# Cross attention: scores of two units as two 64-row products side by side, in place of one 128-row product per unit

## The chip, the cores and the metric

The kernel runs on one core of a Trainium2 chip. The metric is the device time of one execution in microseconds (us), as the median of several runs.

Engines: TensorE (PE in the profile, and PEld for its weight loads), VectorE (DVE), ScalarE (ACT), GpSimd (POOL) and SyncE (SP), which issues transfers.

## The reference, cut to what matters

A decoder of two layers on 8 batches of 256 tokens with 256 features. Each layer has a self mixing part (window attention, then a recurrence), a cross attention over 77 context rows, and a feed-forward part (experts, then a binarized one); each part is followed by a residual sum and a layer norm. Only the two cross attentions are changed. Both compute:

```
Q = (x @ Wq + bq)      # 16 heads of 16 features
K = (ctx @ Wk + bk)    # ctx: 77 rows of 256
V = (ctx @ Wv + bv)
scores = einsum('bhqd,bhkd->bhqk', Q, K) / sqrt(16)    # masked
attn = softmax(scores)
x = layernorm(x + (attn @ V) @ Wo + bo)
```

## The kernel before, in words

`cross_attention` is called twice, for layer 0 and layer 1. It loops over the batches 0 to 7. Batch 0 and batch 7 are written out; the six between are three turns of a loop that holds an odd and an even batch. A batch has 8 units (`UNITS`), `c` = 0 to 7. A unit is 128 of the batch's 256 tokens and 4 of the 16 heads (`UH` = 4): units 0 to 3 are the first 128 tokens, 4 to 7 the second.

Queries and keys lie transposed: features on the 128 partitions, in two halves `g` of 8 heads each. A head has 16 features, so the heads of a product for 4 heads need only 64 of the 128 partitions. The keys are kept once per head in `km`, multiplied by 1 on the head's own 16 partitions and by 0 elsewhere (`mask_keys` on GpSimd). A score product takes 128 partitions of `q` as weights and 4 heads x 77 columns of `km` as the moving operand; the other heads' partitions meet zeros. The operands are fp32, and each fp32 product shows in the profile as two records.

The steps of a unit, by engine:

- TensorE `score` (L1200): scores of 4 heads, 128 x 308, into `s_bank[c % 2]`.
- VectorE `mask_scores` (L1076 in layer 0, L1074 in layer 1) from the bank to `z`; `take_maximum` (L1082).
- GpSimd `subtract` (L953).
- ScalarE `power` (L1017): the exponential, to `probs`.
- TensorE `turn_probs` (L1209): four transposes into a `t_bank`.
- ScalarE (L1025) and VectorE `probs_rest` (L1087) read it out as a high and a low f16 part, `pth` and `ptl`.
- TensorE `weigh` (L1223): the product with the values.

The order on each engine is written out by hand, and every engine works its queue in that order. TensorE's order for unit `c` is: `turn_probs(c)`, `score(c + 2)`, the shared step of slot `c`, `weigh(c - 1)`. VectorE's is: mask of `c + 2`, `probs_rest(c)`, maximum of `c + 2`, then other work. ScalarE's is: copy of turned `c`, exponential of `c + 1`, then the shared step. For `c` = 6 and 7 the scores are those of units 0 and 1 of the next batch.

The shared steps go by slot (`CA`): slot 0 the keys of the next batch (L1175), slot 1 its values (L1179), slot 2 the transposed heads (L1184) and slot 3 the output product (L1189) of the previous batch's second 128 tokens, slot 4 the transposed tokens of the next batch (L1163, read out to `xt` by ScalarE L995), slot 5 its query product (L1169, read out to `q` by ScalarE L998), slots 6 and 7 heads and output of the batch's first 128 tokens.

Window attention, earlier in the kernel, is not changed. Its `score` first writes a band mask with 128-row bf16 products (L678) and then adds fp32 products on 32 rows each (L684), in turn on the four groups of 32 rows; its `weigh` (L714) uses 128 rows again.

Of the kernel before, what the change touches and what calls it, by code (L numbers as in the profile page):

```python
# [27 lines left out]
P = 128  # L28
# [134 lines left out]
def first(b):  # L163

    return isinstance(b, int) and b == 0
# [44 lines left out]
def window_attention(nc, x_dram, xt_dram, wqkv_dram, wo_dram, rope_dram, ident, half, X, next_loads):  # L210
# [561 lines left out]
CTX = 77  # L772
CH, CD = 16, 16
UH = 4
UNITS = TPB * CH // UH
MASKED = -4.0e9
OPEN = 1.0e38
# [11 lines left out]
    first=[("key", 0), ("value", 0), ("tokens", 0), ("query", 0)],  # L789
# [25 lines left out]
def cross_attention(nc, weights, ctx_dram, ident, half, X, next_loads=None, table=None):  # L815
    tag, additive = weights.tag, weights.additive
    w, bias, rows, mask = weights.w, weights.bias, weights.rows, weights.mask
    with ExitStack() as ctx:
# [14 lines left out]
        q = [sb(f"q{k}", [P, KT_, SEQ]) for k in range(2)]  # L833
        kb = sb("kb", [P, KT_, CTX])
        km = [sb(f"km{k}", [P, KT_, CH // KT_, CTX]) for k in range(2)]
        v = sb("v", [P, CH, CD])
        vh = [sb(f"vh{k}", [P, CH, CD + 1], F16) for k in range(2)]
        vl = [sb(f"vl{k}", [P, CH, CD + 1], F16) for k in range(2)]
        z = [sb(f"z{k}", [P, UH, CTX]) for k in range(2)]
        top = sb("top", [P, 2, UH])  # L840
        probs = [sb(f"probs{k}", [P, UH, CTX]) for k in range(2)]
        pth = [sb(f"pth{k}", [P, UH * P], F16) for k in range(2)]
        ptl = [sb(f"ptl{k}", [P, UH * P], F16) for k in range(2)]
        inv = sb("inv", [P, TPB, CH])
# [5 lines left out]
        s_bank = [ctx.enter_context(nc.psum_tensor(f"{tag}_scores{k}", [P, 512], F32)) for k in range(2)]  # L850
# [15 lines left out]
        scores = sem("scores")  # L866
        masked = sem("masked")
# [63 lines left out]
        def _(pool):  # L931
# [18 lines left out]
            def subtract(b, c):  # L950
                pool.wait_ge(maxed, b * UNITS + c + 1)
                k = c % 2
# [93 lines left out]
        def _(dve):  # L1046
            for k in range(2):
                dve.memset(vh[k][:, :, CD:CD + 1], SCALE)
                ins = dve.memset(vl[k][:, :, CD:CD + 1], 0.0)
# [15 lines left out]
            def mask_scores(b, c):  # L1065

                k = c % 2
                dve.wait_ge(scores, b * UNITS + c + 1)
                if not (first(b) and c < 2):
                    dve.wait_ge(exped, b * UNITS + c - 1)  # L1070
                s = s_bank[k][:, 0:UH * CTX].rearrange("p (h k) -> p h k", h=UH)
                m = at(mask if additive else limit, b * TPB + c // (UNITS // TPB)).unsqueeze(1).broadcast_to((P, UH, CTX))
                if additive:
                    ins = dve.scalar_tensor_tensor(out=z[k][:], in0=s, scalar=CD ** -0.5, in1=m, op0=ALU.mult, op1=ALU.add)  # L1074
                else:
                    ins = dve.tensor_tensor(z[k][:], s, m, ALU.min)  # L1076
                ins.then_inc(masked, 1)
# [75 lines left out]
        @block.tensor  # L1153
        def _(pe):
            def step(b, par, kind, i, bank, uses):
                dst = shared[bank]
                if not (isinstance(uses, int) and uses == 0):
                    pe.wait_ge(free[bank], uses)
                if kind == "tokens":
                    pe.wait_ge(staged[par], 8 * (b - par) + 16)  # L1160
                    for g in range(KT_):
                        for t in range(TPB):
                            ins = pe.transpose(dst[:, g * SEQ + t * P:g * SEQ + (t + 1) * P],  # L1163
                                               xs[par][:, t, g * P:(g + 1) * P], ident[:])
                elif kind == "query":
                    wait_read(pe, [("tokens", 0)], b)
                    for g in range(KT_):
                        for k in range(KT_):
                            ins = pe.matmul(dst[:, g * SEQ:(g + 1) * SEQ], w[:, 0, k, g * P:(g + 1) * P], xt[par][:, k],  # L1169
                                            start=(k == 0), stop=(k == KT_ - 1))  # L1170
                elif kind == "key":
                    pe.wait_ge(context_loaded[par], 8 * (b - par) + 16)
                    for g in range(KT_):
                        for k in range(KT_):
                            ins = pe.matmul(dst[:, g * CTX:(g + 1) * CTX], w[:, 1, k, g * P:(g + 1) * P],  # L1175
                                            context[par][:, k], start=(k == 0), stop=(k == KT_ - 1))
                elif kind == "value":
                    for k in range(KT_):
                        ins = pe.matmul(dst[0:CTX, 0:DIM], context[par][:, k], w[:, 2, k],  # L1179
                                        start=(k == 0), stop=(k == KT_ - 1))  # L1180
                elif kind == "heads":
                    pe.wait_ge(normed, b * TPB + i + 1)
                    for g in range(KT_):
                        ins = pe.transpose(dst[:, g * P:(g + 1) * P],  # L1184
                                           o[:, i, g * 8:(g + 1) * 8].rearrange("p h d -> p (h d)"), ident[:])
                else:
                    wait_read(pe, [("heads", i)], b)
                    for g in range(KT_):
                        ins = pe.matmul(dst[:, 0:DIM], ot[:, i, g], w[:, 3, g], start=(g == 0), stop=(g == KT_ - 1))  # L1189
                ins.then_inc(full[bank], 1)  # L1190

            def score(b, c, par):
                t, part = divmod(c, UNITS // TPB)
                g, h = part // 2, UH * (part % 2)
                if c == 0:
                    wait_read(pe, [("query", 0)], b)
                    pe.wait_ge(key_masked, (b + 1) * KT_)
                if not (first(b) and c < 2):
                    pe.wait_ge(masked, b * UNITS + c - 1)
                pe.matmul(s_bank[c % 2][:, 0:UH * CTX], q[par][:, g, t * P:(t + 1) * P],  # L1200
                          km[par][:, g, h:h + UH].rearrange("p h k -> p (h k)"), start=True, stop=True).then_inc(scores, 1)

            def turn_probs(b, c):
                k = c % 2
                pe.wait_ge(exped, b * UNITS + c + 1)
                if not (first(b) and c < 2):
                    pe.wait_ge(probs_low, b * UNITS + c - 1)
                for h in range(UH):
                    ins = pe.transpose(t_bank[k][0:CTX, h * P:(h + 1) * P], probs[k][:, h], ident[:])  # L1209
                ins.then_inc(probs_t, 1)  # L1210

            def weigh(b, c, par):
                k, t = c % 2, c // (UNITS // TPB)
                pe.wait_ge(probs_low, b * UNITS + c + 1)
                if c == 0:
                    pe.wait_ge(v_low, b + 1)
                if c % (UNITS // TPB) == 0 and not first(b):
                    pe.wait_ge(normed, b * TPB + t - 1)
                for h in range(UH):
                    head = UH * (c % (UNITS // TPB)) + h  # L1220
                    cols = slice(h * P, (h + 1) * P)
                    for n, (a, x) in enumerate(((pth[k], vh[par]), (pth[k], vl[par]), (ptl[k], vh[par]))):
                        ins = pe.matmul(o_bank[t][:, head, 0:CD + 1], a[0:CTX, cols], x[0:CTX, head],  # L1223
                                        start=(n == 0), stop=(n == 2))
                ins.then_inc(weighted, 1)

            def batch(b, par, before=True, after=True):
                for c in range(UNITS):
                    turn_probs(b, c)
                    if c < UNITS - 2:  # L1230
                        score(b, c + 2, par)
                    elif after:
                        score(b + 1, c + 2 - UNITS, 1 - par)
                    for kind, i, bank, uses in CA.slot(c, b):
                        d = CA.serves(kind, i)
                        step(b + d, (par + d) % 2, kind, i, bank, uses)
                    if c > 0:
                        weigh(b, c - 1, par)
                    elif before:
                        weigh(b - 1, UNITS - 1, 1 - par)  # L1240

            pe.wait_ge(weights.loaded, 64)
            for kind, i, bank, uses in CA.prologue():
                step(0, 0, kind, i, bank, uses)
            score(0, 0, 0)
            score(0, 1, 0)
            both(batch)(pe)
            weigh(BATCH - 1, UNITS - 1, 1)
            for kind, i, bank, uses in CA.epilogue():
                step(BATCH - 1, 1, kind, i, bank, uses)  # L1250
# [1578 lines left out]
```

## Time and profile before

| | |
|---|---|
| median of 3 runs | 1293.64 us (1292.46 to 1300.71) |
| the profiled execution | 1291.09 us, its span 1289.3 us |
| PE, PEld, DVE, ACT, POOL busy, share of the span | 84%, 68%, 75%, 55%, 30% |
| scores of cross attention (L1200), PE | 256 records, 89.6 us busy, 433 ns mean |
| mean granted TensorE clock | 0.924 of full speed |
| cross attention of layer 0, of layer 1 | some 145 us and 142 us of the span |

The span is from the first to the last record of the profile; the execution's own time is a little longer. A busy PE counts each product's latency too, and products overlap in the pipeline, so 84% does not mean that it has no room. Start times are microseconds from the span's start.

### The profile page before, as it was taken

The page shows a single profiled execution, that of the slowest core. Times are in us where ns is not written, and L with a number is a line of the kernel's source. Part 1 is how long each engine was busy: PE and PEld are TensorE (multiplying, and loading weights), DVE is VectorE, ACT ScalarE, POOL GpSimd, SP SyncE. Part 2 cuts the span into 40 slices and gives each one's busy share as a digit, 9 for nine tenths or more (in the row PEclk, how much of TensorE's full clock was granted, in tenths as well). Part 3 has the DMA queues.
Part 4 walks back from the last instruction along what each step waited for, and adds up shares of the span by engine and source line. Part 5 has one row for each costly group of instructions (what it writes and reads, how often), then busy time and mean ns, then how long its engine had stood idle before and what let it go on. Part 6 is the DMA issues. An engine that isn't in the chain of part 4 may idle for free. (4 is left out here: it accounts for less than half of the span.)

```text
span 1289.3 us, 30260 instructions
## 1 busy us (share of the span) xinstructions
PE 1087.8 (84%) x10763; PEld 881.4 (68%) x10763; DVE 961.6 (75%) x2254; ACT 704.9 (55%) x1459; POOL 388.9 (30%) x538
## 2 busy tenths in 40 slices
PE   4899989999987699986269999389999569999696
PEld 3578878778776577774257777378787447777485
DVE  7587877878875488884938883569998538888497
ACT  2454444444443355552637775368788525655484
POOL 5122222222220355551130000423331225555232
PEclk9899999999999799995559999699999879999799
DMA  6000000100000500005245431300000000000011
GB/s 257 5 10 2 10 12 2 71 3 2 2 2 2 187 23 22 11 9 227 107 135 172 171 108 49 120 17 26 24 9 9 0 24 23 11 21 9 34 50 50
DMA packets 34072, 65.35 MB, mean 51 GB/s; under 512 B 7590, under 2 KB 23334, under 8 KB 30886
## 3 DMA queue, kind: packets, MB, share of 16 engines
q1 hardware_dynamic: 32422, 59.62, 13.2%
q0 software_dynamic: 1536, 4.20, 1.0%
q8 instruction: 73, 1.20, 0.4%
q14 instruction: 41, 0.34, 0.1%
HBM read 43.03 MB, written 12.39 MB: 43 GB/s over the span
## 5 line engine op out<-in xcount | busy, mean ns | idle before, releaser
L953 POOL TENSOR_TENSOR ca_z<-ca_z,ca_top 128x308 f32<-128x308 f32 x128 | 92.7, 724 | 129.8 <-DVE ca_top L1082 129.5
L389 ACT ACTIVATE wa_probs<-wa_scores,wa_minus_top 128x192 f32<-128x192 f32 x256 | 83.3, 437 | 80.6 <-DVE wa_minus_top L477 80.6
L1025 ACT ACTIVATE ca_pth<-ca_turned 77x512 f16<-77x512 f32 x128 | 75.9, 593 | 59.0 <-PE ca_turned L1209 58.4
L348 POOL TENSOR_TENSOR wa_q<-wa_by_cos,wa_by_sin 128x256 f32<-128x256 f32 x32 | 23.4, 732 | 266.3 <-DVE wa_by_sin L472 266.3
L1209 PE MATMUL ca_turned<-ident,ca_probs 128*77 128x128 f32 x512 | 84.1, 287 | 20.6 <-ACT ca_probs L1017 19.5
L400 ACT ACTIVATE wa_pth<-wa_turned 128x384 f16<-128x384 f32 x128 | 58.4, 506 | 73.5 <-PE wa_turned L696 73.5
L1200 PE MATMUL ca_scores<-ca_km,ca_q 128*128 128x308 f32 x256 | 89.6, 433 | 6.0 <-ACT ca_q L998 5.7
L1087 DVE SCALAR_TENSOR_TENSOR ca_ptl<-ca_turned,ca_pth 77x512 f16<-77x512 f32 x128 | 86.7, 677 | 2.6 <-ACT ca_pth L1025 2.6
L1017 ACT ACTIVATE ca_probs<-ca_z 128x308 f32<-128x308 f32 x128 | 58.2, 455 | 44.8 <-POOL ca_z L953 43.8
L621 PE MATMUL wa_scores<-wa_xh,wa_wh 128*128 128x256 f16 x256 | 70.5, 275 | 11.7 <-DVE wa_wl L456 9.7
L477 DVE TENSOR_REDUCE wa_minus_top<-wa_scores 128x2 f32<-128x384 f32 x128 | 62.3, 549 | 21.1 <-PE wa_scores L684 18.9
L696 PE MATMUL wa_turned<-ident,wa_probs 128*128 128x128 f32 x512 | 69.1, 277 | 9.4 <-DVE wa_ptl L525 5.4
L1209 PEld LDWEIGHTS ca_turned<-ident,ca_probs 128*77 128x77 f32 x512 | 56.0, 148 | 26.4 <-ACT ca_probs L1017 22.6
L525 DVE SCALAR_TENSOR_TENSOR wa_ptl<-wa_turned,wa_pth 128x384 f16<-128x384 f32 x128 | 65.0, 549 | 8.6 <-ACT wa_pth L400 8.6
L2385 PE MATMUL re_g<-re_convh,re_w_gh 128*128 128x256 f16 x256 | 69.8, 273 | 1.2 <-DVE re_convl L2280 1.2
L621 PE MATMUL wa_scores<-wa_xl,wa_wh 128*128 128x256 f16 x256 | 70.5, 275 | 0.0
L621 PE MATMUL wa_scores<-wa_xh,wa_wl 128*128 128x256 f16 x256 | 70.4, 275 | 0.0
L2385 PE MATMUL re_g<-re_convl,re_w_gh 128*128 128x256 f16 x256 | 69.8, 273 | 0.0
L2385 PE MATMUL re_g<-re_convh,re_w_gl 128*128 128x256 f16 x256 | 69.8, 273 | 0.0
L696 PEld LDWEIGHTS wa_turned<-ident,wa_probs 128*128 128x128 f32 x512 | 58.1, 142 | 16.4 <-issue 7.5
L2369 PE MATMUL re_in<-re_xt,re_w_in 128*128 128x256 f32 x256 | 61.6, 402 | 9.0 <-ACT re_xt L2150 9.0
L2369 PEld LDWEIGHTS re_in<-re_xt,re_w_in 128*128 128x128 f32 x256 | 51.0, 202 | 18.8 <-issue 7.2
(332 smaller groups left out, 3677.0 us busy)
## 6 DMA issues: line engine op xcount, KB each, us to landing
ex_stage<-in_ew SPq DMA_DIRECT2D x16, 1024.0 KB, 7.0
slots<-slots_zeros SPq DMA_DIRECT2D x10, 512.0 KB, 5.3
ca_xs<-tokens SPq DMA_DIRECT2D x16, 256.0 KB, 2.3
ex_xe<-slots SPq DMA_DIRECT2D x11, 320.0 KB, 3.3
slots<-ex_y SPq DMA_DIRECT2D x9, 320.0 KB
wa_x_stage<-in_xt SPq DMA_DIRECT2D x8, 256.0 KB, 3.0
tokens<-in_x SPq DMA_DIRECT2D x1, 2048.0 KB, 14.8
ca_w<-in_xw SPq DMA_DIRECT2D x2, 1024.0 KB, 5.6
```

Of the source, the lines that this page charges most:

```text
L389: ins = act.activation(probs[2 * (u % 2) + t][:, h, t * WINDOW:t * WINDOW + SPAN], s_bank[i][:, t * SPAN:(t + 1) * SPAN], ACT.Exp, bias=mi ...
L477: dve.tensor_reduce(minus_top[:, g % 2, i], s_bank[i][:, 0:2 * SPAN].rearrange("p (t s) -> p t s", t=2), AX.X, ALU.max, negate=True).then_ ...
L525: dve.scalar_tensor_tensor(out=spans(ptl[k][:]), in0=spans(t_bank[h][:]), scalar=PSCALE, in1=spans(pth[k][:]), op0=ALU.mult, op1=ALU.subtr ...
L621: ins = pe.matmul(bank[:, a * SEQ:(a + 1) * SEQ], weight[:, k, cols], x[:, par, k], start=(m == 0), stop=(m == 3 * KT_ - 1))
L696: ins = pe.transpose(t_bank[h][:, j * SEQ + t * P:j * SEQ + (t + 1) * P], probs[2 * (u % 2) + t][:, h, j * P:(j + 1) * P], ident[:])
L953: pool.tensor_tensor(z[k][:], z[k][:], top[:, k].unsqueeze(2).broadcast_to((P, UH, CTX)), ALU.subtract).then_inc(shift, 1)
L1025: act.activation(pth[k][0:CTX], t_bank[k][0:CTX], ACT.Copy, scale=PSCALE).then_inc(probs_high, 1)
L1087: dve.scalar_tensor_tensor(out=ptl[k][0:CTX], in0=t_bank[k][0:CTX], scalar=PSCALE, in1=pth[k][0:CTX], op0=ALU.mult, op1=ALU.subtract).then ...
L1200: pe.matmul(s_bank[c % 2][:, 0:UH * CTX], q[par][:, g, t * P:(t + 1) * P], km[par][:, g, h:h + UH].rearrange("p h k -> p (h k)"), start=Tr ...
L1209: ins = pe.transpose(t_bank[k][0:CTX, h * P:(h + 1) * P], probs[k][:, h], ident[:])
L2369: ins = pe.matmul(i_bank[s % 2][:, k], w_in[:, g, m * P:(m + 1) * P], xt[:, g], start=(g == 0), stop=(g == KT_ - 1))
L2385: ins = pe.matmul(g_bank[m][:, k], w[:, j, cols], x[par][:, j], start=(n == 0), stop=(n == 3 * HT - 1))
```

## The change

`score` becomes `score_pair`. It is called for even units alone and issues the scores of unit `c` and unit `c + 1` one behind the other. Unit `c` (even) uses heads 0 to 3 of a half, so partitions 0 to 63; unit `c + 1` uses heads 4 to 7, so partitions 64 to 127. Each product takes only these 64 rows of `q` and `km`, and each goes to a bank of its own, as before. One signal is given after the second product, and `mask_scores` waits for pairs. The pair waits until both units before it have been masked. The order of the other steps is the same.

```diff
+HALF = UH * CD
...
             def mask_scores(b, c):
 
                 k = c % 2
-                dve.wait_ge(scores, b * UNITS + c + 1)
+                dve.wait_ge(scores, b * (UNITS // 2) + c // 2 + 1)
...
-            def score(b, c, par):
+            def score_pair(b, c, par):
+
                 t, part = divmod(c, UNITS // TPB)
-                g, h = part // 2, UH * (part % 2)
+                g = part // 2
                 if c == 0:
                     wait_read(pe, [("query", 0)], b)
                     pe.wait_ge(key_masked, (b + 1) * KT_)
-                if not (first(b) and c < 2):
-                    pe.wait_ge(masked, b * UNITS + c - 1)
-                pe.matmul(s_bank[c % 2][:, 0:UH * CTX], q[par][:, g, t * P:(t + 1) * P],
-                          km[par][:, g, h:h + UH].rearrange("p h k -> p (h k)"), start=True, stop=True).then_inc(scores, 1)
+                if not (first(b) and c == 0):
+                    pe.wait_ge(masked, b * UNITS + c)
+                for k in range(2):
+                    rows = slice(HALF * k, HALF * (k + 1))
+                    ins = pe.matmul(s_bank[k][:, 0:UH * CTX], q[par][rows, g, t * P:(t + 1) * P],
+                                    km[par][rows, g, UH * k:UH * (k + 1)].rearrange("p h k -> p (h k)"), start=True, stop=True)
+                ins.then_inc(scores, 1)
...
                 for c in range(UNITS):
                     turn_probs(b, c)
-                    if c < UNITS - 2:
-                        score(b, c + 2, par)
-                    elif after:
-                        score(b + 1, c + 2 - UNITS, 1 - par)
+                    if c % 2 == 0:
+                        if c < UNITS - 2:
+                            score_pair(b, c + 2, par)
+                        elif after:
+                            score_pair(b + 1, 0, 1 - par)
...
-            score(0, 0, 0)
-            score(0, 1, 0)
+            score_pair(0, 0, 0)
```

## Rows read from the trace of the kernel before

**Rows 1.** Busy time by stretches: layer 0, one batch of it, layer 1.

```profile
core 0: us, PE busy (x) PEld busy (x) DVE busy (x) ACT busy (x) POOL busy (x), PEclk, DMA share, GB/s
432.20:577.50 145.30, 133.38 (x1348) 109.04 (x1349) 123.32 (x315) 82.63 (x181) 78.36 (x103) 0.98 0.10 34
489.34:507.87 18.53, 17.41 (x181) 14.31 (x181) 16.32 (x43) 10.95 (x25) 10.58 (x15) 1.00 0.06 20
1052.50:1194.00 141.50, 131.07 (x1349) 107.02 (x1350) 121.18 (x313) 84.01 (x182) 78.47 (x103) 1.00 0.05 15
```

**Rows 2.** Waits, 452.92 to 562.80 us: total, times, longest.

```profile
DVE ca_z L1076 <- PE ca_scores L1200: 8.5, 10, 1.4
```

**Rows 3.** Timeline of TensorE, units 4 to 6 of an odd batch: start, length.

```profile
502.11 0.66 PE L1209 MATMUL ca_turned<-ident,ca_probs 128*77 128x128 f32 x4 [0.21 <-ACT ca_probs L1017]
...
503.13 0.60 PE L1163 MATMUL ca_shared<-ident,ca_xs 128*128 128x128 f32 x4
503.88 0.64 PE L1209 MATMUL ca_turned<-ident,ca_probs 128*77 128x128 f32 x4
...
504.36 0.68 PE L1200 MATMUL ca_scores<-ca_km,ca_q 128*128 128x308 f32 x2
504.88 1.89 PE L1169 MATMUL ca_shared<-ca_xt,ca_w 128*128 128x256 f32 x8
...
507.87 0.78 PE L1200 MATMUL ca_scores<-ca_km,ca_q 128*128 128x308 f32 x2 [0.32 <-ACT ca_q L998]
```

**Rows 4.** Timelines of VectorE and ScalarE in that odd batch.

```profile
495.00 0.48 DVE L1076 TENSOR_TENSOR ca_z<-ca_scores,ca_limit 128x308 f32<-128x308 f32 x1 [0.61 <-PE ca_scores L1200]
...
503.59 0.48 DVE L1076 TENSOR_TENSOR ca_z<-ca_scores,ca_limit 128x308 f32<-128x308 f32 x1
...
508.89 0.48 DVE L1076 TENSOR_TENSOR ca_z<-ca_scores,ca_limit 128x308 f32<-128x308 f32 x1 [1.33 <-PE ca_scores L1200]
...
503.77 0.60 ACT L995 ACTIVATE ca_xt<-ca_shared 128x512 f32<-128x512 f32 x1
```

**Rows 5.** Timeline of TensorE, units 0 to 2 of an even batch.

```profile
512.25 0.68 PE L1200 MATMUL ca_scores<-ca_km,ca_q 128*128 128x308 f32 x2
...
513.92 0.64 PE L1209 MATMUL ca_turned<-ident,ca_probs 128*77 128x128 f32 x4
...
516.09 0.64 PE L1209 MATMUL ca_turned<-ident,ca_probs 128*77 128x128 f32 x4
516.57 0.68 PE L1200 MATMUL ca_scores<-ca_km,ca_q 128*128 128x308 f32 x2
```

**Rows 6.** Timelines of ScalarE and VectorE in that even batch.

```profile
514.60 0.59 ACT L1025 ACTIVATE ca_pth<-ca_turned 77x512 f16<-77x512 f32 x1 [0.16 <-PE ca_turned L1209]
515.34 0.46 ACT L1017 ACTIVATE ca_probs<-ca_z 128x308 f32<-128x308 f32 x1
...
512.97 0.48 DVE L1076 TENSOR_TENSOR ca_z<-ca_scores,ca_limit 128x308 f32<-128x308 f32 x1
...
515.52 0.68 DVE L1087 SCALAR_TENSOR_TENSOR ca_ptl<-ca_turned,ca_pth 77x512 f16<-77x512 f32 x1
...
517.45 0.47 DVE L1076 TENSOR_TENSOR ca_z<-ca_scores,ca_limit 128x308 f32<-128x308 f32 x1
```

**Rows 7.** Window attention: timeline of TensorE, and the first 32-row records (ns, min/median/max).

```profile
300.00 0.81 PE L678 MATMUL wa_scores<-wa_band,wa_ident_bf 128*128 128x384 bf16 x4
...
300.49 0.33 PE L678 MATMUL wa_scores<-wa_band,wa_ident_bf 128*128 128x384 bf16 x1
300.75 1.58 PE L684 MATMUL wa_scores<-wa_k,wa_q 32*128 32x192 f32 x32
302.26 0.20 PE L714 MATMUL wa_out<-wa_vh,wa_pth 128*128 128x65 f16 x1
...
L684 PE MATMUL wa_scores<-wa_k,wa_q x4: 425/425/425, 300.7 to 300.8; 32*128 32x192 f32 x4
L684 PE MATMUL wa_scores<-wa_k,wa_q x32: 321/321/425, 300.7 to 302.0; 32*128 32x192 f32 x32
```

**Rows 8.** Timelines of ScalarE and TensorE at the start of layer 0.

```profile
428.60 0.60 ACT L995 ACTIVATE ca_xt<-ca_shared 128x512 f32<-128x512 f32 x1 [1.72 <-PE ca_shared L1163]
...
429.34 0.89 PE L1169 MATMUL ca_shared<-ca_xt,ca_w 128*128 128x256 f32 x3 [0.78 <-ACT ca_xt L995]
```

## The prediction

> **What bounds the kernel now.** I first read the table by stretches of time [rows 1]. The change touches only the two cross attentions, 145.3 and 141.5 us of a span of 1289.3 us, and in both TensorE has its full clock (0.98 and 1.00 of 2.4 GHz). TensorE looks fullest there: 17.41 of the 18.53 us of one batch. But that time counts each product's latency too. VectorE is busy for 16.32 us of the same batch, so there are 2.2 us per batch, at most, that a faster TensorE could give back.
>
> Next the waits [rows 2]. In 110 us VectorE waits for scores 8.5 us, in ten waits. So most masks don't wait for a score product, and the question is which do. For that I read single rows of one odd batch [rows 3, 4] and one even batch [rows 5, 6] of the loop. I call turn(c), score(c), mask(c) and exp(c) the steps of unit c. The pattern repeats in all inner batches, with periods of 18.5 and 18.2 us in turn.
>
> The even units form a ring: turn(c), score(c+2), mask(c+2), maximum, subtraction, exp(c+2), turn(c+2), of some 4.2 us. At its end turn waits for exp: turn(4) starts at 502.11 after 0.21 us idle on ScalarE [rows 3]. The odd units' turns come without a wait, straight behind the preceding work of TensorE (503.88, no idle). Once per batch the ring is replaced by a longer path: score(6), the transposed tokens at 503.13, xt on ScalarE at 503.77, the query product at 504.88, q, then score(0) of the next batch at 507.87, which waited for ScalarE, and mask(0) at 508.89 after 1.33 us idle [rows 3, 4].
>
> **What the change takes away.** Two records of one score take 0.68 us, and the next work starts 0.52 us after the score's start (504.36 to 504.88) [rows 3]. The change issues each odd unit's product next to the even one's. If the two run at once, TensorE is relieved of 0.52 us in each odd unit, 64 times in both attentions: 33 us of TensorE.
>
> Do they run at once? Window attention has the nearest rows: fp32 products on 32 of the 128 rows, 32 records of 192 columns, last 1.58 us [rows 7]. Taken one after the other, at a column rate of 0.52 us / 616 (that is, two records of 308), they would last 32 x 192 x 0.52/616 = 5.2 us. So four ran at once, and two groups of 64 rows should do so too. That is my value; the bound on the other side is no overlap, another 0.52 us per pair.
>
> **What it adds.** A pair has to change TensorE over from 128 rows to 64 and back, which the score before didn't. What such a change costs is seen in window attention [rows 7]. On entry: the last 128-row record starts at 300.49, the 32-row ones at 300.75, 0.26 us later. The 128-row records themselves start (0.81 - 0.33)/3 = 0.16 us apart: 0.10 us lost. The first four records take 425 ns where 321 is the median: another 0.10, because their weights weren't loaded during earlier work. A score that starts after a wait shows the same (0.78 us at 507.87 against 0.68) [rows 3]. On exit: the last 32-row record starts at 300.75 + 1.58 - 0.32 = 302.01, the next work at 302.26. That is 0.25 us, against the 0.16 that 192 columns take (192 x 0.52/616): 0.09 lost. The next operation's load isn't hidden either. Its price lies between 0 and 0.08 us (a query product behind a wait: three records in 0.89 us, against 0.38 + 2 x 0.216 = 0.81, the stride of 0.216 being (1.89 - 0.38)/7 from the steady eight) [rows 3, 8]; I take 0.06. So scores come 0.20 us later than now in each even unit, work behind them 0.35 us later, and work of the next odd unit 0.35 - 0.52 = 0.17 us earlier.
>
> TensorEngine Tiling (Array Packing), Key Properties, of the Trainium skill says that changing the tiling mode drains TensorE; the 0.10 and 0.09 us above agree. By that rule alone there is no size; with nothing lost at the change-over the time would be that of the second rival.
>
> The new wait, for mask(c+1) before the pair (c+2, c+3), costs nothing. The pair (0, 1) at 507.87 needs mask(7), which comes two VectorE instructions after mask(6) at 503.59, and those last under 0.7 us each [rows 3, 4]; the other pairs lie the same way. Behind that wait would be queued the rest of TensorE's unit. The halved count of score signals and the missing zero padding cost nothing either: a product costs its columns, 308 as before.
>
> **Where 0.20 and 0.35 us land.**
> - Unit 2, even batch: score(2) ends at 512.25 + 0.68 = 512.93 and mask(2) starts 0.04 us later, so 0.04 is the signal's latency, and mask(2) moves by 0.20 [rows 5, 6]. exp(2) ends at 515.34 + 0.46 = 515.80, turn(2) starts at 516.09 [rows 5, 6], behind TensorE's own work. There are 0.24 us of slack: turn(2) doesn't move, or gains 0.04. In the odd batch mask(2) starts at 495.00, after 0.61 us idle, longer than the even batch's signal needs [rows 4]. I put that down to the loop's branch, as the even batch doesn't have it. Cost 0; if it is the score that it waits for, 0.20.
> - turn(1) comes 0.35 us later, so the copy of its result (514.60) ends at 515.54 and the remainder of probabilities at 515.52 becomes 515.58: VectorE, which is back to back there, loses 0.06 [rows 5, 6].
> - Unit 4: score(4) ends at 517.25, mask(4) starts at 517.45, so with the latency there are 0.16 us of slack. The 0.20 less the 0.04 gained fits; mask(4) moves by the 0.06 of above, or by 0.04 where nothing was gained [rows 5, 6]. I take 0.06 for every batch.
> - Unit 6: score(6) ends 503.29, mask(6) starts 503.59: 0.25 us of slack hide the 0.20 [rows 3, 4].
> - The path to the next batch, where the gain should be. The query product would start 0.52 us earlier, but the pair (6, 7) stands ahead of the tokens' transposes. They end 0.35 us later, xt starts at 504.12 and ends at 504.72. In the first batch the query product started 429.34 - (428.60 + 0.60) = 0.14 us after xt [rows 8], so here at 504.86, against 504.88 now. Its load is no longer hidden: 0.08. The path is 0.06 us longer, and nothing is gained.
> - score(0) waits for q now and pays the unhidden load already (0.78 us); as a pair its end moves by one start offset, 0.01.
>
> Sum per batch: 0.06 + 0.06 + 0.01 = 0.13 us; 16 batches, the first and last counted like the others: +2.1 us. The 33 us of TensorE turn into idle time ahead of the turns of even units, which wait for exp.
>
> **Forecast.** The profiled execution took 1291.1 us (span 1289.3 and 1.8 around it), so the sum gives 1293.2. The median of the runs shown is 2.6 us above the profiled execution, and the changed kernel's time is such a median too, which would give 1295.8. I give 1295; the rivals' times below have the 2.6 in them. About 1% (13 us) is what a measurement of this kernel can tell from no change.
>
> **Rivals.**
> 1. The two products don't overlap. The pair ends another 0.52 us later, 0.72 in all, which no slack holds. Odd batch: mask(2) 0.25 (0.72 less some 0.47 of its idle 0.61), mask(4) 0.56, query path 0.58, score(0) 0.52: 1.9 us. Even batch: turn(2) 0.48, then the same three: 2.1. Times 16: +32 us, 1326. Against it stands window attention [rows 7], for it only that 64-row groups aren't shown. Half an overlap (the second record of the first product holds up the second product) is 0.26 in place of 0.52: odd 0 + 0.30 + 0.32 + 0.26, even 0.22 more, 1.0 us on average, +16, 1310. The point at which a slower kernel can be told is 0.8 us per batch.
> 2. The change-over is free. Then only odd units change. The query product starts when xt ends plus latency, 504.37 + 0.14, and pays 0.08: 0.29 us gained. Even batch: turn(2) gains its 0.24 and mask(4), whose score and VectorE queue both move up, some 0.35. Odd 0.29 and even 0.64, on average 0.47, times 16: -7.5 us, 1286. The records of window attention speak against it [rows 7].
> 3. TensorE is the bound, by its 17.41 us of 18.53. Then all 33 us come off: 1261. Against it: VectorE's 16.32 us and turns that wait for exp. TensorEngine Tiling (Array Packing), Theoretical Speedup, of the Trainium skill promises up to 2x for contractions of 64 or fewer, which is this rival's result if TensorE were alone.
>
> **Chances.** Forecast 0.73; no overlap 0.08; half overlap 0.05; free change-over 0.10; TensorE as the bound 0.02; 0.02 for something else. Faster by over 1%: 0.03; slower: 0.08 + 0.05, and 0.01 of the rest, 0.14; within 1%: 0.83. The range takes in the forecast and the free change-over, and above it the odd batch's mask(2) at 0.20 for 8 batches (1.6 us) and turns of twice my size, short of the half overlap: 1284 to 1304. That leaves out 0.17.
>
> **What would show it.** In the changed profile: score records of 64 rows in fours, two starting within 0.02 us; a gap of some 0.21 us between the last turn record and the pair (0.11 now); a tail of about 0.35 us; mask(0) still with over 1 us idle; periods of 18.3 to 18.7 us. TensorE's busy time falls while VectorE's stays. The prediction is wrong if xt isn't on the path, if the pairs' records start 0.26 us apart, or if the granted clock of these stages falls below 0.98.

## The result, and the profile after

The changed kernel takes 1306.7 us (median of 13 runs, 1301.0 to 1311.4), the one before, timed alongside, 1295.8 us (13 runs, 1290.8 to 1301.1). The ratio is 1.0084 with a 95% interval of 1.0062 to 1.0106: slower by 11 us. The ratio is just inside the 1% that I called no change (its interval reaches just over it), and the time is outside my range, which ended at 1304. The profiled execution took 1305.3 us, its span is 1303.6.

Busy time of the changed kernel by stretches, with the columns of [rows 1]: batch 0 of layer 0, an odd inner batch, batch 0 of layer 1.

```profile
430.25:454.05 23.80, 18.26 (x129) 12.87 (x129) 13.71 (x29) 8.80 (x21) 8.44 (x11) 0.71 0.26 89
491.01:509.80 18.79, 16.58 (x180) 12.76 (x181) 16.11 (x42) 10.97 (x25) 10.64 (x15) 1.00 0.06 19
1058.70:1078.56 19.86, 15.86 (x129) 11.42 (x129) 12.12 (x27) 10.19 (x22) 8.44 (x11) 0.83 0.00 1
```

The two batches 0 of the kernel before, the same columns:

```profile
432.23:452.92 20.69, 16.09 (x129) 12.96 (x129) 13.72 (x29) 9.05 (x21) 8.46 (x11) 0.84 0.39 138
1052.53:1069.36 16.83, 13.69 (x129) 10.90 (x129) 12.20 (x27) 10.32 (x22) 8.47 (x11) 1.00 0.00 1
```

The inner batch is 0.26 us longer than before (18.53 in [rows 1]). The six inner batches of layer 1 run from 1078.56 to 1190.00, 111.4 us, where before they run from 1069.36 to 1179.26, 109.9 us; both kernels are at full clock there (1.00). Each batch 0 is 3.1 us longer, and its granted clock (the column PEclk, a mean of the two levels 1.2 and 2.4 GHz) is 0.71 in place of 0.84, and 0.83 in place of 1.00. My sum had nothing of that.

Where batch 0 of layer 1 loses its time can be read at once. First the stretch from turn(0) to turn(2), before and then after, and then the two records of turn(0):

```profile
1055.67:1059.66 3.99, 3.99 (x36) 3.35 (x36) 2.42 (x5) 2.43 (x6) 1.05 (x2) 1.00 0.00 0
1061.85:1068.62 6.77, 6.77 (x37) 5.05 (x37) 2.71 (x6) 2.42 (x6) 1.04 (x2) 0.54 0.00 0
```

```profile
1055.67 0.66 PE L1209 MATMUL ca_turned<-ident,ca_probs 128*77 128x128 f32 x4 [1.83 <-ACT ca_probs L1017]
1061.85 1.14 PE L1214 MATMUL ca_turned<-ident,ca_probs 128*77 128x128 f32 x4 [2.36 <-ACT ca_probs L1018]
```

In both kernels turn(0) starts 3.1 us into the batch. Before it TensorE stands idle for 1.83 us in the kernel before and for 2.36 us in the changed one, whose first two products take 0.79 us in place of 1.30. In the changed kernel the clock falls during that wait, and the stretch behind it takes 6.77 us in place of 3.99, nearly all of it at 1.2 GHz: 2.8 of the 3.0 us. The rest of the batch, mostly at full clock again, takes 9.94 us in place of 9.70.

The last batch of each layer, to the end of its layer norm, before and then after:

```profile
562.80:591.50 28.70, 19.69 (x208) 15.02 (x208) 20.37 (x56) 10.54 (x23) 10.15 (x16) 0.89 0.00 1
1179.26:1207.70 28.44, 19.45 (x208) 14.95 (x208) 20.37 (x56) 10.54 (x23) 10.16 (x16) 0.92 0.01 2
```

```profile
565.50:595.30 29.80, 19.71 (x208) 14.24 (x208) 20.44 (x56) 10.66 (x23) 10.21 (x16) 0.86 0.00 1
1190.00:1221.10 31.10, 21.33 (x208) 15.07 (x208) 20.51 (x56) 10.52 (x23) 10.19 (x16) 0.79 0.01 1
```

1.1 and 2.7 us longer, again at a lower clock. So of these two profiles' difference in cross attention, 3.1 us (twice 1.6) lie in the twelve inner batches, and 10 us in the four outer ones (6.1 in the batches 0, 3.8 in the last). From the column PEclk (twice what it lacks to 1, times the length) the four outer batches spent some 18 us at 1.2 GHz before and 42 us after.

Timelines of the changed kernel, the pair of unit 2 (units 4 and 5, for mask(4)) and units 4 to 6 of that odd inner batch, which answer to [rows 3, 4], and the same pair and mask of the even batch behind it, which answer to [rows 5, 6]: TensorE first, then VectorE.

```profile
500.18 0.79 PE L1204 MATMUL ca_scores<-ca_km,ca_q 64*128 64x308 f32 x4
...
504.04 0.66 PE L1214 MATMUL ca_turned<-ident,ca_probs 128*77 128x128 f32 x4 [0.76 <-ACT ca_probs L1018]
504.63 0.79 PE L1204 MATMUL ca_scores<-ca_km,ca_q 64*128 64x308 f32 x4
505.35 0.66 PE L1164 MATMUL ca_shared<-ident,ca_xs 128*128 128x128 f32 x4
506.15 0.64 PE L1214 MATMUL ca_turned<-ident,ca_probs 128*77 128x128 f32 x4
...
509.80 0.79 PE L1204 MATMUL ca_scores<-ca_km,ca_q 64*128 64x308 f32 x4 [0.33 <-ACT ca_q L999]
...
518.68 0.79 PE L1204 MATMUL ca_scores<-ca_km,ca_q 64*128 64x308 f32 x4
```

```profile
501.15 0.48 DVE L1077 TENSOR_TENSOR ca_z<-ca_scores,ca_limit 128x308 f32<-128x308 f32 x1 [0.15 <-PE ca_scores L1204]
...
505.51 0.48 DVE L1077 TENSOR_TENSOR ca_z<-ca_scores,ca_limit 128x308 f32<-128x308 f32 x1
...
519.64 0.48 DVE L1077 TENSOR_TENSOR ca_z<-ca_scores,ca_limit 128x308 f32<-128x308 f32 x1
```

The four records of a pair last 0.79 us, as long as one score that pays for its unhidden load: the two products run at once. The turn of unit 4 now waits 0.76 us for the exponential, where it waited 0.21 [rows 3]: the time that TensorE was relieved of went into such waits. And the path from turn(4) to the next batch's pair is 509.80 - 504.04 = 5.76 us, as before (507.87 - 502.11).

### The profile page after: what moved, and what is told of

It is laid out like the page before. It is cut to its first block and busy times, and to the rows that moved or that the text cites. A ratio compares the mean times of both kernels' runs of the same rounds, so it can differ in the third digit from the quotient of the medians.

```text
span 1303.6 us, 30284 instructions
## 1 busy us (share of the span) xinstructions
PE 1086.5 (83%) x10763; PEld 863.6 (66%) x10763; DVE 961.4 (74%) x2254; ACT 704.1 (54%) x1459; POOL 388.8 (30%) x538
## 5 line engine op out<-in xcount | busy, mean ns | idle before, releaser
L1214 PE MATMUL ca_turned<-ident,ca_probs 128*77 128x128 f32 x512 | 87.4, 296 | 36.0 <-ACT ca_probs L1018 36.0
L477 DVE TENSOR_REDUCE wa_minus_top<-wa_scores 128x2 f32<-128x384 f32 x128 | 62.3, 548 | 20.5 <-PE wa_scores L684 18.5
L2374 PEld LDWEIGHTS re_in<-re_xt,re_w_in 128*128 128x128 f32 x256 | 51.2, 203 | 18.5 <-issue 6.8
L1840 DVE SCALAR_TENSOR_TENSOR ex_hl<-ex_h,ex_hh 128x320 f16<-128x320 f32 x72 | 35.2, 488 | 38.0 <-ACT ex_h L1812 37.3
```

Source lines behind the costliest of these rows:

```text
L477: dve.tensor_reduce(minus_top[:, g % 2, i], s_bank[i][:, 0:2 * SPAN].rearrange("p (t s) -> p t s", t=2), AX.X, ALU.max, negate=True).then_ ...
L2374: ins = pe.matmul(i_bank[s % 2][:, k], w_in[:, g, m * P:(m + 1) * P], xt[:, g], start=(g == 0), stop=(g == KT_ - 1))
```

## The experiments

Ratios are to the kernel before, timed alongside, with 95% intervals. For most kernels I also give the time of the inner batches of layer 0, even and odd or all six, from the profile (before 18.2 and 18.5, six of them 109.9; changed 18.5 and 18.8, six 111.5), since both layers agree within 0.1 us and run at full clock.

**1. The order alone.** Pairs on 128 rows.

```diff
                 for k in range(2):
-                    rows = slice(HALF * k, HALF * (k + 1))
-                    ins = pe.matmul(s_bank[k][:, 0:UH * CTX], q[par][rows, g, t * P:(t + 1) * P],
-                                    km[par][rows, g, UH * k:UH * (k + 1)].rearrange("p h k -> p (h k)"), start=True, stop=True)
+                    ins = pe.matmul(s_bank[k][:, 0:UH * CTX], q[par][:, g, t * P:(t + 1) * P],
+                                    km[par][:, g, UH * k:UH * (k + 1)].rearrange("p h k -> p (h k)"), start=True, stop=True)
```

> The changed kernel with its pairs, but each product on all 128 rows against the zero-padded keys: the order and the signals of the change alone, no 64-row product, no change-over. The two products then follow one another, so the pair ends 0.52 us later than a single score. Theory A (two costs: the ring of the even units is lengthened by what a pair ends later, some 4 us in all, and the rest, some 7 us, is TensorE at half clock in the first and last batches): inner batches 19.5 to 19.8 us (0.26 on unit 4 becomes 0.5, query path 0.2, score(0) 0.5), the mean granted clock back at 0.92 or more, total 1310 to 1316. Theory B (all of the loss is the order of the queue, the clock is by the way): also slow, but with batch 0 at least as long as in the changed kernel, 23.8 us, and the clock at 0.917 or less.

1326.8 us (4 runs), ratio 1.0232 (1.0195 to 1.0268). Inner batches 19.8 and 20.0 us, six of them 119.1. A pair that ends 0.52 us later than a score costs 1.5 us per batch, more than either theory had. The clock did not come back: 0.914 in the profile and 0.917 over the four runs (changed 0.914, before 0.921), batches 0 at 0.78 and 0.77. Theory A missed the clock and the total; theory B had the clock, but batch 0 took 23.1 us, not 23.8 or more. What stands: the lateness of the pair is dear, and the side-by-side products of the change, their change-over paid, save 20 us against the same order without them.

**2. The rows alone.** The kernel before, each score on its own 64 rows.

```diff
-                pe.matmul(s_bank[c % 2][:, 0:UH * CTX], q[par][:, g, t * P:(t + 1) * P],
-                          km[par][:, g, h:h + UH].rearrange("p h k -> p (h k)"), start=True, stop=True).then_inc(scores, 1)
+                rows = slice(h * CD, (h + UH) * CD)
+                pe.matmul(s_bank[c % 2][:, 0:UH * CTX], q[par][rows, g, t * P:(t + 1) * P],
+                          km[par][rows, g, h:h + UH].rearrange("p h k -> p (h k)"), start=True, stop=True).then_inc(scores, 1)
```

> The kernel before with its order (one score per unit, ahead by two), each product on its own 64 rows: the row change alone. TensorE changes over to 64 rows and back in each unit, twice as often as in the changed kernel. Theory A: score 0.20 us later and the work behind it 0.35 us later in each unit; inner batches 19.2 to 19.5 us, total 1309 to 1315. Theory B (the order costs, not the rows): inner batches stay at 18.2 and 18.5 us and the total within 3 us of before.

1338.2 us (4 runs), ratio 1.0351 (1.0317 to 1.0385). Inner batches 19.9 us, 1.4 to 1.6 us above before, for eight change-overs each way. Theory B falls, and theory A had too little (19.2 to 19.5 us, 1309 to 1315 in all). And the clock, which I had left open, fell to 0.903 in the profile. Batch 0 of layer 0 and batch 0 of layer 1:

```profile
430.82:460.47 29.65, 25.84 (x129) 16.50 (x129) 13.80 (x29) 8.86 (x20) 8.73 (x11) 0.55 0.28 96
1071.82:1099.49 27.67, 25.32 (x129) 16.18 (x129) 12.29 (x27) 10.15 (x21) 8.74 (x11) 0.57 0.00 1
```

Both batches 0 ran almost wholly at 1.2 GHz and took 9 to 11 us longer than before, with the same columns in TensorE and TensorE busy 87% of the time or more. The six inner batches, from 460.47 to 580.00, were at 0.99 to 1.00.

**3. 64-row pairs only in the inner batches.**

```diff
-                    rows = slice(HALF * k, HALF * (k + 1))
+                    rows = slice(0, P) if isinstance(b, int) else slice(HALF * k, HALF * (k + 1))
```

> The changed kernel, but pairs of batches 0 and 7 and the first pair of batch 1, which are written out, use 128 rows; inner batches keep their 64-row pairs at 18.5 and 18.8 us. Theory A: TensorE is kept busier in the first batches, their half-clock stretches shrink to those of before (batch 0 of layer 0 falls from 23.8 us to 21 or 22, that of layer 1 from 19.9 to 17 or 18), mean clock 0.922 or more, total 1299 to 1302. Theory B: pairs one after the other only lengthen batch 0 further, total 1306 to 1311.

1311.1 us (6 runs), ratio 1.0123 (1.0097 to 1.0149). At the upper end of theory B (1306 to 1311). Batches 0 took 23.2 and 22.1 us at a clock of 0.78 and 0.77. These batches had 128-row products only, as in experiment 1, and yet a lower clock than the kernel before: so it isn't the 64 rows alone that cost clock. The pair's order costs clock without them.

**4. A filler in the outer batches** of the changed kernel, which adds work that isn't part of the computation.

```diff
+                if c % 2 == 0 and isinstance(b, int):
+                    pe.matmul(o_bank[t][:, :, CD + 1:32], ident[:], q[par][:, 0, 0:240].rearrange("p (h d) -> p h d", h=CH),
+                              start=True, stop=True)
                 for h in range(UH):
                     head = UH * (c % (UNITS // TPB)) + h
```

> The changed kernel, with one more fp32 product of 240 columns on 128 rows ahead of the weighing of each even unit in batches 0 and 7, into columns of the output bank that nobody reads: added work that is not part of the computation. It stands in odd units, where the change took 0.52 us of TensorE away, and takes 0.4 us. Theory A: the granted clock in batches 0 stays higher, batch 0 of layer 0 takes 21 to 22.5 us in place of 23.8 and that of layer 1 17 to 18.5 in place of 19.9; total 1300 to 1303. Theory B: added work gives nothing back, 1306 to 1308.

1300.9 us (10 runs), ratio 1.0045 (1.0026 to 1.0064), against 1.0084 without: added work takes 5 to 6 us off. In the profile batch 0 of layer 0 takes 21.8 us at 0.84, the last batches 28.8 and 28.5 us as in the kernel before; but batch 0 of layer 1 takes 20.8 us at 0.84, no better than without. The trace shows why: there too turn(0) follows 2.36 us of idle time and takes 0.95 us in place of 0.66, so the clock has fallen already, and the first filler stands behind turn(1). Its mean granted clock over the runs is 0.926; the changed kernel's is 0.914, that of before 0.921.

**5. The filler's control:** the same lines in the kernel before.

> The control for the filler: the kernel before with the same 240-column product in batches 0 and 7, into columns that nobody reads. In the changed kernel the filler took 5.8 us off. Theory A (the pairs lost clock that the filler gives back): here there is less to give back; 0.4 us of work in each even unit of the outer batches against little or no half clock, -1 to +3 us. Theory B (the filler helps any kernel, as all spend time at half clock ahead of and in batch 0): it takes 4 to 6 us off here too.

1295.8 us (12 runs), ratio 1.0002 (0.9981 to 1.0023). Theory A. The mean clock rose here too, from 0.921 to 0.924, but batches 0 took 21.2 and 17.3 us in place of 20.7 and 16.8: what the filler gave in clock it cost in work. In the changed kernel it gave 5 to 6 us more than it cost. With experiment 4 this shows that a part of the loss is granted clock. With the filler in both kernels the medians are still 5 us apart; in the two profiles the inner batches differ by 3.1 us and batch 0 of layer 1, where the filler comes too late, by 3.5.

**6. Score ahead of the turn**, one per unit on 128 rows.

```diff
-                    turn_probs(b, c)
                     if c < UNITS - 2:
                         score(b, c + 2, par)
-                    elif after:
-                        score(b + 1, c + 2 - UNITS, 1 - par)
+                    elif c == UNITS - 1 and after:
+                        score(b + 1, 1, 1 - par)
+                    turn_probs(b, c)
+                    if c == UNITS - 2 and after:
+                        score(b + 1, 0, 1 - par)
```

> The kernel before (one score per unit, 128 rows), but TensorE's order within units 0 to 5 is score of c + 2 first and then the turning of c, and in unit 7 too; unit 6 stays. TensorE now computes the score while it waits for the exponential, so a score is off the ring of the even units. Theory A (a ring of waits sets the period): the ring falls from 4.2 us to some 3.8 us (turn 0.66, copy 0.59, remainder 0.68, maximum 0.46, subtraction 0.70, exponential 0.46 and the signals), less than VectorE's own work then allows; inner batches 17.4 to 18.0 us, total 1283 to 1290. Theory B (TensorE's work sets it, or VectorE's already does): order changes nothing, 18.2 and 18.5 us, within 3 us of before.

1289.6 us (12 runs), ratio 0.9960 (0.9943 to 0.9977), inner batches 17.8 and 18.4, six of them 108.3 us. Faster, and within theory A's total; the even batch gained 0.4 us, the odd one only 0.1. TensorE works as much as before (104.3 us busy in the six batches, 104.4 before), so the ring of waits, not TensorE's work, set the period.

**7. Pair ahead of the turn:** the change, with its pair in the other place.

```diff
-                    turn_probs(b, c)
-                    if c % 2 == 0:
-                        if c < UNITS - 2:
-                            score_pair(b, c + 2, par)
-                        elif after:
-                            score_pair(b + 1, 0, 1 - par)
+                    if c % 2 == 0 and c < UNITS - 2:
+                        score_pair(b, c + 2, par)
+                    turn_probs(b, c)
+                    if c == UNITS - 2 and after:
+                        score_pair(b + 1, 0, 1 - par)
```

> The changed kernel with its 64-row pairs, but the pair of c + 2 and c + 3 is issued ahead of the turning of c instead of behind it (units 0, 2 and 4; unit 6 stays). Theory A: the change-over and the later end of the pair fall into TensorE's wait for the exponential and leave the ring, so inner batches fall from 18.5 and 18.8 us to that of the one-score version of this order or up to 0.2 us below, 17.3 to 18.0; what remains as a loss is the half-clock time in the outer batches; total 1288 to 1298. Theory B (the change-over costs wherever it stands): inner batches stay within 0.1 us of 18.5 and 18.8.

1289.7 us (12 runs), ratio 0.9944 (0.9924 to 0.9964), against 1.0084 in the place of the change. The six inner batches of layer 0 of this kernel, and two records of its timeline in unit 4:

```profile
455.77:562.20 106.43, 99.20 (x1080) 77.56 (x1080) 95.35 (x252) 64.38 (x145) 64.20 (x85) 1.00 0.06 19
...
503.02 0.79 PE L1204 MATMUL ca_scores<-ca_km,ca_q 64*128 64x308 f32 x4
503.74 0.66 PE L1214 MATMUL ca_turned<-ident,ca_probs 128*77 128x128 f32 x4
```

The pair lasts 0.79 us here too, and the turn follows 0.72 us behind its start: the change-over costs what it did, but in front of a turn that would have waited. 106.4 us is 5.1 less than with the change's order and 3.5 less than before. Theory B falls. But the order alone, with single scores, had brought it to 108.3 us (experiment 6): the pair adds 1.9 us per layer to that, and in the whole kernel no difference to 0.9960 can be told.

**8. Pair ahead of the turn, 128 rows everywhere.** Experiment 7 with the edit of experiment 1.

> Pair ahead of the turn with 128-row products everywhere: the order of the fast version without the 64-row products. What 64 rows are worth once the order is right. Theory A (in this order TensorE's time begins to matter, so the 0.52 us per pair shows, at least in the query path where unit 6 still has it behind the turn): inner batches 18.2 to 18.8 us, total 1293 to 1300. Theory B (the order does it all, the rows nothing): 17.6 and 18.1 us as with 64 rows, 1286 to 1290.

1305.3 us (12 runs), ratio 1.0071 (1.0047 to 1.0094), inner batches 18.6 and 19.2, six of them 113.0 us. Against experiment 7 the two products side by side are worth 6.6 us per layer in the inner batches. Theory B falls, and theory A's total (1293 to 1300) was too low. The order isn't all: a pair needs them.

**9. Three more on the clock.** The filler with the score ahead; the filler with the pair ahead; and the pair ahead with 128 rows in the outer batches.

> Score ahead of the turn, one per unit on 128 rows, and the filler in batches 0 and 7. Theory A: 0 to 3 us below the same order without the filler, 1282 to 1288. Theory B: as that kernel or above it.

> The changed kernel with the pair ahead of the turn, and the filler product of 240 columns in batches 0 and 7 into columns that nobody reads. Pair ahead of the turn alone had inner batches of 17.6 and 18.1 us and 221 us at half clock; before has 198. Theory A (the clock in the outer batches is a cost of its own): inner batches unchanged, half-clock time back to some 195 us, 2 to 6 us below the version without the filler: 1284 to 1288. Theory B: the filler gave something back only where the ring was long; here 0 to +2 us, 1289 to 1292.

> Pair ahead of the turn, 64 rows in the inner batches, but 128 rows (two products one after the other) in batches 0 and 7 and for the first pair of batch 1. Theory A: with the pair in TensorE's waiting time its length hurts little, and 128-row work holds the clock better: 0 to 4 us below the all-64-row version, 1286 to 1290. Theory B (as in the changed kernel, where this edit cost 4 us): the longer pair lengthens the outer batches more than the clock gives back: 1290 to 1294.

The first took 1288.0 us, ratio 0.9953 (0.9933 to 0.9973); without the filler it was 0.9960: no difference to be told. The second took 1289.3 us, ratio 0.9943 (0.9922 to 0.9964), without 0.9944: theory A missed. The mean clock rose from 0.918 to 0.921, but its batches 0 took 20.6 and 18.0 us, where without the filler they took 20.4 and 17.4: the filler cost what the clock gave. The third took 1291.9 us, ratio 0.9970 (0.9949 to 0.9992), theory B's number, though its interval overlaps that of experiment 7: the longer pair in the outer batches brings nothing, and may cost some 2 us.

**What clock is worth.** Within one kernel the runs differ mostly by their clock: the 13 of the changed kernel lie between 1301.0 us at 0.923 and 1311.4 us at 0.906. A straight line through them falls by 5.7 us per 0.01; one through the 79 runs of the kernel before in the experiments falls by 8.1. The means are 0.9144 and 0.9206, so by these lines the difference is worth 3.5 to 5.0 us of the 11 between the kernels. That is an estimate: it takes clock lost by a change to cost what clock lost by chance does, and in experiment 5 the clock rose and the time did not fall, as it was bought with added work.

## Why the prediction was wrong

By its own steps:

- **The two products run at once:** right. Four records in 0.79 us, and experiment 1 shows what it would be otherwise. The rival of no overlap and that of half an overlap both fall. The second would have given 1310, near the measured time, by a mechanism that isn't there. That experiment 1 took 1326.8 us, the first rival's 1326, is luck as well: its inner batches lost 1.5 us each and not 2.0, and the rest lay in the outer ones.
- **The change-over's price:** right. The pair starts 0.59 us after the turn (0.50 before) and lasts 0.79 (0.68 before), that is 0.20; the tokens' transposes start 0.72 us after it in place of 0.52 and take 0.66 in place of 0.60. From turn(4) to turn(5) it is 2.11 us, before 1.77: 0.34, where I had 0.35. The rival of a free change-over falls.
- **The query path, unit 6, the wait for mask(c+1):** right, to 0.06 us. From turn(4) to score(0) it is 5.76 us before and after, where I had 5.82. mask(6) starts 0.09 us behind the pair's end, without a wait. No pair waits for a mask.
- **Unit 4:** wrong, and this is the term that sizes the inner batches. I allowed mask(4) 0.16 us of slack, by taking a signal's latency of 0.04 us from mask(2). After the change the pair ends at 500.18 + 0.79 = 500.97 and mask(4) starts at 501.15, now waiting 0.15 us for it: its latency is 0.18, nearly the whole distance that I took for slack. In the even batch it is 519.64 - (518.68 + 0.79) = 0.17, where before it was 517.45 - 517.25 = 0.20: 0.03 us of slack in place of 0.16. So the pair's lateness reaches the ring in full. Counted from score(0), mask(4) of the even batch moves from 9.58 to 9.84 us, and that is the whole 0.26 us of the batch: turn(2) starts 0.07 us later, where I had it unmoved, the pair ends another 0.22 us later, and the slack takes up 0.03. In my sum the slack hid the pair, and mask(4) moved only by the 0.06 us of VectorE's queue. In place of 0.13 us per batch it is 0.26. mask(4) is where the token tile and so the row of `limit` changes, with an index worked out from a register inside the loop; in batch 0, where it is a constant, mask(4) of the kernel before starts 0.04 us behind its score. That this is the cause of the longer latency wasn't tried.
- **The outer batches count like the others:** wrong, and the larger error. I read rows of inner batches, all at full clock, and gave batches 0 and 7 the same 0.13 us. In the profiles they hold 10 of the 13 us that cross attention's batches lost. Most of it comes with the clock: some 24 us more at 1.2 GHz in the four batches, 5.6 us that came back in experiment 4 (2.0 in batch 0 of layer 0, 1.0 and 2.6 in the last batches), and 2.8 us in the one slow stretch of batch 0 of layer 1. I had taken the clock for full because [rows 1] gave 0.98 and 1.00, but those stretches end at 577.50 and 1194.00, some 14 us before the last batches do, and the 0.98 hides a stretch at 1.2 GHz in batch 0.
- **TensorE as the bound:** falls, by experiment 6.

The chain is then, of the 13 us in the profiles' cross attentions: inner batches 0.26 x 12 = 3.1 us (measured in both layers, at full clock); the same 0.26 or so in each outer batch, about 1 us; and what is left, some 9 us, with more time at 1.2 GHz in the outer batches. The new slow stretches follow waits for the exponential that the change made longer: 2.36 us in place of 1.83 in batch 0 of layer 1, 1.30 in place of 0.81 at turn(4) of batch 0 of layer 0, 1.29 in place of 0.97 at turn(2) of layer 1's last batch. What stays open is which wait brings the clock down and which doesn't (layer 0's last batch had 1.28 us at the same turn and kept its clock there), and the share of clock and of order within a slow stretch. I had a sentence on a falling clock among what would make the prediction wrong, but no rival and no chance for it, though batch 0 of layer 0 was at half clock for a part of its time in the kernel before too.

## What to carry to other kernels

Relieving an engine pays only where its instructions stand between two waits that matter; first look whether the instruction sits on the ring, and whether it could be issued while the engine waits anyway. Here the kernel with the pair was 0.8% slower than before with the pair behind the turn and 0.6% faster with it ahead; 0.4% came from that order alone, without a pair. Side-by-side products are worth their change-over when it falls into a wait. And when TensorE's work is cut, price the first and last batches too, where it waits most, at both clocks, and not only the full inner loop.

## What the runs showed of the hardware

- Two fp32 products on 64 rows each, on different halves of the array and with different banks, start within 0.01 us (two records at 504.63, 0.52 us each) and take no longer together than one. At full clock, going from 128 rows to 64 and back costs TensorE 0.2 us on the way in (0.09 of it before the first record starts, the rest as an unhidden weight load) and 0.14 to 0.15 us on the way out.
- With single 64-row scores TensorE stayed at 1.2 GHz for almost the whole of batch 0 in both layers (granted clock 0.55 and 0.57), though it was busy 25.84 of 29.65 us and 25.32 of 27.67; the kernel before, with the same columns on 128 rows and TensorE busy 16.09 of 20.69 us, had 0.84. Once at full clock, in the inner batches, it stayed there. What of the 64-row work does this, these runs don't tell.
- Where VectorE waited for a score, its mask started 0.04 to 0.05 us behind the score's end in some units (unit 2 of even batches, unit 4 of batch 0) and 0.17 to 0.27 us in others of the same code (unit 4 of inner batches 0.17 to 0.18, unit 0 0.24 to 0.27).
